# Eight products moved from GpSimd to VectorE, and the ramp's stores and a reciprocal reordered

## The chip, the cores and the metric

The kernel runs on one core of one Trainium2 chip. Its engines are TensorE (PE; its weight loads are PEld), VectorE (DVE), ScalarE (ACT), GpSimd (POOL) and SyncE (SP, which here only issues DMAs). Each works through its own list of instructions in program order and waits on semaphores for the others. The metric is the device time of one execution in microseconds (us), lower is better; several runs are given as a median.

## The reference, cut to what matters

```python
x = x + ln(attn_ref(ln(x), ...))      # x: 16 batches of 256 tokens, 128 channels
x = x + ln(ffn_ref(ln(x), ...))       # ln: layer norm without weights

def attn_ref(x, ...):                 # 8 heads of 16 channels
    Q, K, V = x @ Wq + bq, x @ Wk + bk, x @ Wv + bv
    qq, kq = Q @ Wc2q + bc2q, K @ Wc2q + bc2q             # 8 values per head
    fid = (qq @ kq.T) / maximum(norm(qq) * norm(kq), 1e-8)
    qw = fid * (1 + 0.1 * sin(fid * pi))
    aw = 0.5 * qw + 0.5 * (Q @ K.T) / sqrt(16)
    x1 = layernorm(x + (softmax(aw) @ V) @ Wo + bo, g1, beta1)
    qm = (x1 @ W1 + b1) @ Wm + bm
    ff = ((tanh(qm) * cos(qm * pi / 4)) @ Wqo + bqo) @ W2 + b2
    return layernorm(x1 + ff, g2, beta2)

def ffn_ref(x, ...):                  # 8 experts; each token goes to one
    probs = softmax(x @ gate_w); e = argmax(probs)
    return probs[e] * (gelu(x @ w1[e] + b1[e]) @ w2[e] + b2[e])
```

## The kernel before

The 4096 tokens are 32 tiles of 128, tile by tile in the partitions: 16 batches of two tiles for the attention, 8 groups of four tiles (g = 0 to 7) for the work behind it, in two halves h = 0 and 1. Every engine's program is one function, and the order of the calls in it is the order of work; nothing plans it.

**Setup and ramp.** Projections, the norms of the quantum features `u`, and for each batch b two round trips through HBM that lay operands out anew, issued from SyncE: `put_qk(b)` and `get_qk(b)` for the parts of Q and K, `put_u(b)` (four stores) and `get_u(b)` (two loads) for the features, and `put_max(b)` and `get_max(b)` for the negated maxima of the logits' rows, which TensorE needs before `logit_unit(1)` of the batch. A `get` waits until its `put` has landed. The reciprocal roots of the norms come in two parts: part 0 for batches 0 to 3, part 1 for the rest; in `reciprocals(hh)` VectorE inverts ScalarE's root (L1724), and in `root_out(hh)` GpSimd refines it in four instructions (L701 to L704) and raises `inv_h`.

**The batch loop.** For each batch VectorE runs four `weight` (L1850), two `logits` (L1880), four `top` for the batch after next (L1827) and `heads` of the batch before. TensorE's output goes round three PSUM slots, so a unit waits until the unit three places earlier is taken. GpSimd runs `split_max` (L739, L741), `split_u`, `split_qk` and a subtraction; in batch 0 `root_out(1)` stands last, and `reciprocals(1)` behind VectorE's four `top`.

**Behind the attention.** For each group g, TensorE makes the block's output, ScalarE squares it (`square_z(g)`, L1037), VectorE's `weigh(g)` (L1966, L1968) writes `t` into `u_sb`, and two sums over the channels are wanted for each token: of t squared (`square_t`, L1054, and `sum_t`) and of t times x. The product is `times_x(g)`: 128x512, into one of two buffers `tx`. For groups 0 to 3 VectorE sums it (`sum_dot(g)`, L2024); for 4 to 7 ScalarE does (`dot_x(g)`, L1063, four accumulating passes). `dots(h)` needs the sums of a half. Then VectorE makes roots (`newton`, L1996 to L1999), variances (`var_o`, L1977 to L1986), gates, the choice of the expert (`best`), places in the sorted list (`places`), and rows (`add_shift` L2012, `add_x` L2020).

**The experts.** GpSimd scatters 32 tiles of rows by indirect DMA (L828), each group when its `add_x` is done. `list_tiles` on VectorE makes the list of tiles (`exp_i`); from it ScalarE and SyncE load weights (L1173) and rows, and 23 steps of matmuls, GELU and layer norm follow.

## Time and profile before

| | |
|---|---|
| median of 3 runs | 507.27 us (504.33 to 507.42) |
| the profiled execution | 505.17 us, span 503.4 us |
| busy share of the span | PE 75%, DVE 74%, ACT 66%, POOL 49% |
| chain that ended last, by engine | DVE 39%, PE 33%, issue 11%, DMA 5%, POOL 4%, ACT 3% |
| mean granted TensorE clock | 0.884 of full speed |

The span runs from the first to the last instruction; the profiled execution's own time holds 1.77 us more. In the order of time: setup and ramp until VectorE's first `weight` at 69.65 us, batches 0 and 1 until 103.18 us, fourteen more batches until 278 us, the work behind the attention until 373.7 us, the experts until the end. In a timeline row, `[1.08 <-PE ...]` is the time that the engine had stood idle and whose work ended that; "issue" means that it waited for nothing that the profile shows. Rows of instructions that follow one another are merged (x4).

### The profile page before, as it was taken

Reading aid. Unit: us, or ns where it says so; the run is one execution under the profiler, and the core shown is the slowest. Engines: PE = TensorE matmul, PEld = TensorE weight load, DVE = VectorE, ACT = ScalarE, POOL = GpSimd, SP = SyncE. Lnnn points to the kernel's source line nnn. Section 1 sums busy time; section 2 is a strip of 40 time slices with the busy share of each in tenths; the row PEclk is TensorE's granted clock in tenths of the full one; section 3 lists DMA queues with packets and bytes.
Section 4 is the critical chain, followed back from the end, with each engine's and each line's share of the span. In section 5 each row is a group of like instructions: output and inputs, shape, how many; then the busy total and the mean of one; then the engine's idle time right before and its main releaser. Section 6 shows DMA issues by size and latency. Waiting matters only on the chain.

```text
span 503.4 us, 8868 instructions
## 1 busy us (share of the span) xinstructions
PE 377.1 (75%) x2644; PEld 264.6 (53%) x2644; DVE 372.5 (74%) x910; ACT 333.4 (66%) x635; POOL 245.3 (49%) x348
## 2 busy tenths in 40 slices
PE   1967368899999999998888898640004599999960
PEld 0755236566656666665575336440003488888840
DVE  5496587799999999999965344997982057776781
ACT  1357347699999999999866456656203287778730
POOL 7469131755555555554201224216477147766773
PEclk9998758799999999999888999976557599999995
DMA  9416344366776776676599910000128346766400
GB/s 203 16 31 158 94 90 106 97 166 165 169 174 149 175 182 170 163 170 158 143 134 146 148 22 1 2 0 23 35 73 247 106 119 198 206 208 195 136 14 0
DMA packets 87979, 60.33 MB, mean 120 GB/s; under 512 B 17213, under 2 KB 80705, under 8 KB 87926
## 3 DMA queue, kind: packets, MB, share of 16 engines
q1 hardware_dynamic: 78022, 52.07, 46.9%
q10 hardware_dynamic: 7408, 3.35, 2.7%
q0 software_dynamic: 2496, 4.29, 2.4%
q8 instruction: 23, 0.38, 0.3%
q14 instruction: 30, 0.25, 0.2%
HBM read 35.38 MB, written 25.21 MB: 120 GB/s over the span
## 4 chain that ended last, share of the span: by engine, by line
DVE 39%; PE 33%; issue 11%; DMA 5%; POOL 4%; ACT 3%; SPq 2%; ACTq 1%; POOLq 0%; DVEq 0%
DVE big L1850 11%; DVE mxs L1827 10%; PE ps L1635 8%; PE ps L1626 7%; DVE big L1880 4%; PE ps L1418 2%; PE ps L1431 2%; PE ps L1528 2%; PE ps L1523 1%; PE ps L1411 1%; PE ps L1223 1%; DVE u_sb L1889 1%; DMA qk_parts<-proj 1%; DVE gb L1698 1%; DMA uk_parts<-u_turned 1%
## 5 line engine op out<-in xcount | busy, mean ns | idle before, releaser
L1850 DVE SCALAR_TENSOR_TENSOR big<-big,ps 128x1024 f32<-128x1024 f32 x64 | 74.2, 1215 | 4.4 <-ACT big L954 4.4
L1827 DVE TENSOR_REDUCE mxs<-ps 128x4 f32<-128x1024 f32 x64 | 74.1, 1216 | 4.5 <-issue 2.8
L954 ACT ACTIVATE big<-ps 128x1024 f32<-128x1024 f32 x64 | 62.4, 1028 | 11.3 <-PE ps L1396 11.1
L842 POOL DMA_INDIRECT out_dram<-arena,fidx x46 | 46.5, 1010 | 25.3 <-DVE arena L2246 17.9
L2218 DVE TENSOR_SCALAR arena<-ps,x_all 128x128 f32<-128x128 f32 x46 | 14.0, 347 | 46.3 <-PE ps L1643 34.4
L1626 PE MATMUL ps<-arena,big 128*128 128x256 f32 x184 | 45.4, 392 | 1.1 <-issue 1.1
L1635 PE MATMUL ps<-arena,big 128*128 128x256 f32 x184 | 45.8, 393 | 0.5 <-ACT arena L1162 0.5
L1144 ACT ACTIVATE x_all<-x_all 128x128 f32<-128x128 f32 x46 | 20.3, 489 | 37.0 <-DMA x_all<-sorted_rows 30.1
L1258 PE MATMUL ps<-arena 96*128 96x256 bf16 x256 | 39.3, 285 | 7.2 <-issue 4.8
L828 POOL DMA_INDIRECT sorted_rows<-proj,sl_i x32 | 32.6, 1020 | 21.9 <-issue 15.5
L1880 DVE TENSOR_TENSOR big<-big,ps 128x1024 f32<-128x1024 f32 x32 | 37.9, 1216 | 6.9 <-PE ps L1418 6.9
L739 POOL CAST mtok<-mxs 128x16 bf16<-128x16 f32 x16 | 3.2, 198 | 81.5 <-DVE mxs L1827 81.5
L1162 ACT ACTIVATE arena<-ps,eb_sb 128x256 f32<-128x256 f32 x92 | 36.1, 475 | 7.4 <-PE ps L1626 3.7
L1626 PEld LDWEIGHTS ps<-arena,big 128*128 128x128 f32 x184 | 36.3, 198 | 7.0 <-issue 1.7
L1418 PE MATMUL ps<-arena 98*128 98x256 bf16 x256 | 38.6, 286 | 1.3 <-DMA arena<-m_parts 1.3
L1411 PE MATMUL ps<-ident,big 128*128 128x128 f32 x256 | 36.5, 288 | 2.8 <-DVE big L1850 2.5
L1431 PE MATMUL ps<-big,vb 128*32 128x256 f32 x512 | 36.9, 409 | 1.9 <-DVE u_sb L1889 1.1
L1635 PEld LDWEIGHTS ps<-arena,big 128*128 128x128 f32 x184 | 34.1, 196 | 5.5 <-ACT arena L1162 1.0
L964 ACT ACTIVATE big<-ps 128x1024 f32<-128x1024 f32 x32 | 32.8, 1024 | 6.1 <-PE ps L1418 5.9
L1411 PEld LDWEIGHTS ps<-ident,big 128*128 128x128 f32 x256 | 29.3, 146 | 9.2 <-DVE big L1850 5.9
L1258 PEld LDWEIGHTS ps<-arena 96*128 96x128 bf16 x256 | 23.0, 100 | 17.7 <-issue 14.1
L964 ACT ACTIVATE big<-big 128x1024 f32<-128x1024 f32 x32 | 32.2, 1059 | 0.0
(350 smaller groups left out, 893.0 us busy)
## 6 DMA issues: line engine op xcount, KB each, us to landing
big<-in_L_ffn_w_dram SPq DMA_DIRECT2D x34, 256.0 KB
qk_parts<-proj SPq DMA_DIRECT2D x16, 384.0 KB, 3.0
arena<-qk_parts SPq DMA_DIRECT2D x32, 192.0 KB, 3.7
sorted_rows<-zrow SPq DMA_DIRECT2D x16, 266.0 KB, 5.7
arena<-qk_parts SPq DMA_DIRECT2D x32, 128.0 KB, 3.9
big<-in_L_ffn_w_dram ACTq DMA_DIRECT2D x12, 256.0 KB
x_all<-sorted_rows SPq DMA_DIRECT2D x23, 133.0 KB
sorted_rows<-zrow SPq DMA_DIRECT2D x2, 1263.5 KB, 24.5
```

Source lines behind the costliest of these rows:

```text
L842: nc.gpsimd.indirect_dma_start(out2, bass.IndirectOffsetOnAxis(ap=fidx[:, j, t:t + 1], axis=0), fres[j][:, t, :], None, bounds_check=NT * ...
L954: nc.scalar.activation(W[par][:, n, :], src, ACT.Sin, scale=PI * (1 - 1e-6)).then_inc(sin_ready, 1)
L964: nc.scalar.activation(W[par1][:, n, :], src, ACT.Exp, scale=0.05).then_inc(p_ready, 1)
L1258: mm = nc.tensor.matmul(o[:, c:c + S], cqT[b1 % 3][0:KC, 2 * n + h, qt * P:(qt + 1) * P], ckT[b1 % 3][0:KC, 2 * n + h, :], start=True, sto ...
L1411: nc.tensor.matmul(o[:, to:to + P], W[par][:, n, at:at + P], ident[:, :], is_transpose=True, start=(kt == 0 and qt == 0), stop=False, skip ...
L1418: mm = nc.tensor.matmul(o[:, c:c + S], ckT[i3][0:KC + 2, 2 * n + h, kt * P:(kt + 1) * P], cqT[i3][0:KC + 2, 2 * n + h, :], start=not turn, ...
L1431: mm = nc.tensor.matmul(hbank[32 * j:32 * j + 32, g * S:(g + 1) * S], vb[:, b1 * TPB + kt, h * VW:h * VW + 32], W[par1][:, h // 2, c:c + S ...
L1626: mm = nc.tensor.matmul(ps[:, 1 + 2 * par + c // 2, (c % 2) * TS:(c % 2 + 1) * TS], fw1[s % DEPTH][:, c * P:(c + 1) * P], fxT[par], start= ...
L1635: mm = nc.tensor.matmul(ps[:, 5 + 2 * par, 0:TS], fw2[s % DEPTH][:, c, :], fg[par][:, c, :], start=(c == 0), stop=(c == EC - 1))
L1827: nc.vector.tensor_reduce(mxs[:, b1 % 2, :, 2 * n:2 * n + 2], src, AX_X, ALU.max, negate=True).then_inc(unit_free, 1)
L1850: nc.vector.scalar_tensor_tensor(W[par][:, n, :], W[par][:, n, :], 10.0, f, ALU.add, ALU.mult).then_inc(unit_free, 1)
L1880: nc.vector.tensor_tensor(W[par][:, n, :], W[par][:, n, :], slot_of("log", b, n), ALU.add).then_inc(unit_free, 1)
```

## The change

Four edits. On SyncE the four stores of `put_u(1)` move ahead of `get_u(0)`, and `put_qk(2)` ahead of `get_u(1)`. On VectorE `reciprocals(1)` moves from behind batch 0's `top` to ahead of its first `weight`. `times_x` becomes a VectorE instruction: the eight calls leave GpSimd's program (where six stood ahead of the scatters and two between the first four and the others) and are spread over VectorE's. On ScalarE `dot_x(4)` moves ahead of `square_t(5)` and `dot_x(5)` ahead of `square_t(6)`; `dot_x(4)` also waits until `sum_t(3)` has read the buffer that it writes to.

```diff
             put_u(0)
+            put_u(1)
             get_u(0)
-            put_u(1)
+            put_qk(2)
             get_u(1)
-            put_qk(2)
             get_qk(2)
...
-            for g in range(GH + 2):
-                times_x(g)
             pool.wait_ge(z_stored, 16 * (NB + 4))
-            scatter(0, 0, GT)
-            times_x(GH + 2)
-            times_x(GH + 3)
-            scatter(0, GT, NK)
+            scatter(0, 0, NK)
...
             def dot_x(g):
                 act.wait_ge(step["tx"], g + 1)
+                if g == GH:
+                    act.wait_ge(step["tred"], GRED[GH - 1])
...
             turn_qe(7)
+            dot_x(4)
             square_t(5)
             exps(0)
             nc.scalar.activation(hT[:, 3:4], halfpi[:, 0:1], ACT.Sqrt)
             square_z(6)
+            dot_x(5)
             square_t(6)
...
             square_t(7)
-            dot_x(4)
-            dot_x(5)
             half_root(4, 5, step["vc"], step["rc"], 1)
...
                     for n in range(HP):
                         top(1, n)
+                    reciprocals(1)
...
-                if first:
-                    reciprocals(1)
...
+            def times_x(g):
+                dve.wait_ge(step["t"], 2 * g + 2)
+                if g >= GH + 2:
+                    dve.wait_ge(step["dot"], g - GH - 1)
+                elif g >= 2:
+                    dve.wait_ge(step["tred"], GDOT[g - 2])
+                nc.vector.tensor_tensor(tx[g % 2].rearrange("p (t c) -> p t c", t=GT), t_of(g), x_all[:, g * GT:(g + 1) * GT, :], ALU.mult).then_inc(step["tx"], 1)
...
             fold(1)
+            times_x(0)
             weigh(1)
             sum_t(0)
             weigh(2)
             queries(1)
+            times_x(1)
             sum_dot(0)
...
             sum_t(2)
+            times_x(2)
             sum_t(3)
+            times_x(3)
             var_o(0)
...
             sum_dot(3)
+            times_x(4)
             dots(0)
...
             weigh(5)
+            times_x(5)
             newton(6, 7, step["rd"], 0)
...
             weigh(6)
+            times_x(6)
             weigh(7)
+            times_x(7)
             var_z(1)
```

SyncE in the ramp, from behind the stores of `put_u(0)`; the digit of a name is its buffer, here the batch, and `qk_parts0` on L499 is the store of batch 2. Before:

```order
L530 DMA proj<-uq_parts0 128x1x512
L530 DMA proj<-uk_parts0 128x1x512
L507 DMA uq_parts1<-u_turned1 64x2x256
L508 DMA uk_parts1<-u_turned1 64x2x256
L507 DMA uq_parts1<-u_turned1 64x2x256
L508 DMA uk_parts1<-u_turned1 64x2x256
L530 DMA proj<-uq_parts1 128x1x512
L530 DMA proj<-uk_parts1 128x1x512
L499 DMA qk_parts0<-proj 128x6x256
```

and now:

```order
L507 DMA uq_parts1<-u_turned1 64x2x256
L508 DMA uk_parts1<-u_turned1 64x2x256
L507 DMA uq_parts1<-u_turned1 64x2x256
L508 DMA uk_parts1<-u_turned1 64x2x256
L530 DMA proj<-uq_parts0 128x1x512
L530 DMA proj<-uk_parts0 128x1x512
L499 DMA qk_parts0<-proj 128x6x256
L530 DMA proj<-uq_parts1 128x1x512
L530 DMA proj<-uk_parts1 128x1x512
```

Both loads of the features now stand behind batch 1's stores, and the store of batch 2's Q and K stands two loads further ahead.

VectorE in batch 0 (`weight`, `logits`, `top`) and at the start of batch 1. Before:

```order
L1827 TENSOR_REDUCE mxs<-ps 128x2x2 x6
L1850 SCALAR_TENSOR_TENSOR big<-big,ps 128x1024 x4
L1880 TENSOR_TENSOR big<-big,ps 128x1024 x2
L1827 TENSOR_REDUCE mxs<-ps 128x2x2 x4
L1724 RECIPROCAL inv<-inv 128x384
L1850 SCALAR_TENSOR_TENSOR big<-big,ps 128x1024 x4
```

and now:

```order
L1816 TENSOR_REDUCE mxs<-ps 128x2x2 x6
L1713 RECIPROCAL inv<-inv 128x384
L1839 SCALAR_TENSOR_TENSOR big<-big,ps 128x1024 x4
L1869 TENSOR_TENSOR big<-big,ps 128x1024 x2
L1816 TENSOR_REDUCE mxs<-ps 128x2x2 x4
L1839 SCALAR_TENSOR_TENSOR big<-big,ps 128x1024 x4
```

The reciprocal has moved from the end of batch 0 to its beginning, ten instructions up.

VectorE behind the attention, from the last instruction of `weight_out(0)` to the first of `add_shift(1)`. Before:

```order
L2097 RECIPROCAL proj<-rs 128x16
L1966 TENSOR_TENSOR u_sb<-ps,vec_bc 128x512
L1968 COPY late_s<-ps 128x40
L1966 TENSOR_TENSOR u_sb<-ps,vec_bc 128x512
L1968 COPY late_s<-ps 128x40
L1972 SCALAR_TENSOR_TENSOR late_s<-late_s 128x16
```

and now:

```order
L2093 RECIPROCAL proj<-rs 128x16
L1954 TENSOR_TENSOR u_sb<-ps,vec_bc 128x512
L1956 COPY late_s<-ps 128x40
L2024 TENSOR_TENSOR arena<-u_sb,x_all 128x512
L1954 TENSOR_TENSOR u_sb<-ps,vec_bc 128x512
L1956 COPY late_s<-ps 128x40
L2024 TENSOR_TENSOR arena<-u_sb,x_all 128x512
L1960 SCALAR_TENSOR_TENSOR late_s<-late_s 128x16
```

A product (`arena<-u_sb,x_all`) now follows each of `weigh(6)` and `weigh(7)`; all other instructions keep their order.

## Rows read from the trace of the kernel before

**Rows 1.** Windows: stretch us, length, busy us (instructions) per engine, TensorE clock, DMA share, GB/s.

```profile
69.65:87.85 18.20, 13.85 (x98) 8.85 (x97) 14.13 (x12) 13.57 (x17) 6.40 (x10) 0.72 0.44 93
...
87.85:103.18 15.33, 12.49 (x94) 8.55 (x94) 12.03 (x13) 10.76 (x14) 10.01 (x17) 0.78 0.42 106
...
103.18:115.20 12.02, 11.43 (x114) 7.41 (x110) 11.99 (x14) 11.96 (x15) 6.51 (x12) 1.00 0.70 177
...
307.35:373.70 66.35, 22.07 (x136) 17.32 (x134) 57.14 (x204) 32.80 (x153) 28.08 (x26) 0.71 0.06 18
```

**Rows 2.** Timeline of VectorE, batches 0 and 1: start us, us, instruction, idle before.

```profile
79.73 1.22 DVE L1880 TENSOR_TENSOR big<-big,ps 128x1024 f32<-128x1024 f32 x1 [2.19 <-PE ps L1418]
...
85.39 2.54 DVE L1724 RECIPROCAL inv<-inv 128x384 f32<-128x384 f32 x1
...
93.48 1.22 DVE L1880 TENSOR_TENSOR big<-big,ps 128x1024 f32<-128x1024 f32 x1 [1.08 <-PE ps L1418]
...
96.89 1.22 DVE L1880 TENSOR_TENSOR big<-big,ps 128x1024 f32<-128x1024 f32 x1 [2.19 <-PE ps L1418]
```

**Rows 3.** Timeline of the other engines and SyncE's queue, 53 to 92 us.

```profile
53.38 0.58 SPq L530 DMA_DIRECT2D proj<-uq_parts  x1
...
60.91 0.42 SPq L499 DMA_DIRECT2D qk_parts<-proj  x1
...
69.90 0.42 SPq L536 DMA_DIRECT2D m_parts<-mrow  x1
...
75.26 1.01 PE L1418 MATMUL ps<-arena 98*128 98x256 bf16 x4 [1.29 <-DMA arena<-m_parts]
...
85.02 2.83 ACT L954 ACTIVATE big<-ps 128x1024 f32<-128x1024 f32 x3
...
88.01 0.83 POOL L701 TENSOR_TENSOR gb<-inv 128x384 f32<-128x384 f32 x1 [10.16 <-DVE inv L1724]
...
91.55 0.20 POOL L739 CAST mtok<-mxs 128x16 bf16<-128x16 f32 x1
```

**Rows 4.** Source view of the product's line on GpSimd: duration ns min/median/max.

```profile
L817 POOL TENSOR_TENSOR arena<-u_sb,x_all x8: 1263/1270/1275, 308.2 to 348.4; 128x512 f32<-128x512 f32 x8
```

**Rows 5.** Groups of VectorE from 307 to 373 us: busy us, mean ns.

```profile
L2020 DVE SCALAR_TENSOR_TENSOR proj<-u_sb,late_s,x_all 128x128 f32<-128x128 f32 x20 | 6.7, 397 | 0.1
...
L2012 DVE SCALAR_TENSOR_TENSOR u_sb<-u_sb,late_s,be2c_bc 128x128 f32<-128x128 f32 x20 | 5.6, 342 | 0.0
...
L1966 DVE TENSOR_TENSOR u_sb<-ps,vec_bc 128x512 f32<-128x512 f32 x8 | 5.4, 680 | 9.5 <-ACT gb L1037 9.5
...
L1997 DVE TENSOR_TENSOR late_s<-late_s 128x16 f32<-128x16 f32 x6 | 3.1, 521 | 0.2
...
L1999 DVE SCALAR_TENSOR_TENSOR late_s<-late_s 128x16 f32<-128x16 f32 x6 | 2.0, 334 | 0.2
...
L1985 DVE TENSOR_SCALAR late_s<-late_s,bg_bc 128x16 f32<-128x16 f32 x2 | 1.4, 712 | 0.1
...
L1945 DVE TENSOR_TENSOR late_s<-late_s,bA_bc 128x128 f32<-128x128 f32 x1 | 1.3, 1258 | 0.0
...
L1972 DVE SCALAR_TENSOR_TENSOR late_s<-late_s 128x16 f32<-128x16 f32 x2 | 1.1, 551 | 0.0
...
L1998 DVE SCALAR_TENSOR_TENSOR late_s<-late_s 128x16 f32<-128x16 f32 x6 | 1.1, 183 | 0.2
```

**Rows 6.** Timeline, 314 to 375 us, all engines.

```profile
314.20 0.69 DVE L1966 TENSOR_TENSOR u_sb<-ps,vec_bc 128x512 f32<-128x512 f32 x1 [1.82 <-ACT gb L1037]
...
341.05 0.31 ACT L1054 ACTIVATE arena<-u_sb 128x128 f32<-128x128 f32 x1 [2.62 <-DVE late_s L1968]
...
343.38 0.69 DVE L1966 TENSOR_TENSOR u_sb<-ps,vec_bc 128x512 f32<-128x512 f32 x1 [2.36 <-ACT gb L1037]
...
360.87 0.96 POOL L828 DMA_INDIRECT sorted_rows<-proj,sl_i  x1 [5.17 <-DVE proj L2020]
...
374.71 0.39 ACTq L1173 DMA_DIRECT2D big<-in_L_ffn_w_dram  x1
```

More of the change, by code:

```diff
@@ L809, in _ @@
             std_y(1)
-            def times_x(g):
-                pool.wait_ge(step["t"], 2 * g + 2)
-                if g >= GH + 2:
-                    pool.wait_ge(step["dot"], g - GH - 1)
-                elif g >= 2:
-                    pool.wait_ge(step["tred"], GDOT[g - 2])
-                nc.gpsimd.tensor_tensor(tx[g % 2].rearrange("p (t c) -> p t c", t=GT), t_of(g), x_all[:, g * GT:(g + 1) * GT, :], ALU.mult).then_inc(step["tx"], 1)
             def scatter(k, lo=None, hi=None):
```

## Prediction

> **What bounds the kernel now.** I first cut the span into stretches with the windows view, to see which engine fills each. A regular batch, the one from 103.18 to 115.20 us, takes 12.02 us and keeps VectorE busy for 11.99 of them and ScalarE for 11.96, with TensorE at its full clock [rows 1]. The two batches before it are longer, 18.20 and 15.33 us, though VectorE's work in them is 14.13 and 12.03 us, and TensorE's granted clock is 0.72 and 0.78 of full speed there, between its two levels of 1.2 and 2.4 GHz. So in the ramp VectorE waits. Behind the attention, from 307.35 to 373.70 us, VectorE is busy 57.14 of 66.35 us and every other engine under half: the stage is one chain on VectorE. The change touches these two places.
>
> Next I read VectorE's timeline in the ramp for what it waits for. In batch 0 it waits 2.19 us for the logits from TensorE, and at the end it spends 2.54 us on the reciprocal. In batch 1 it waits 1.08 and 2.19 us, both for TensorE's logits [rows 2]; these 3.27 us are nearly all of the 3.31 by which batch 1 exceeds a regular one. The other engines tell why. In batch 0, TensorE's first logit unit waits for the row maxima from HBM until 75.26 us, whose store SyncE issued at 69.90, behind the long queue of loads. In batch 1, GpSimd begins `root_out(1)` at 88.01, having idled 10.16 us for the reciprocal, and only then, at 91.55, starts `split_max(2)`, which batch 1's first logit unit needs [rows 3].
>
> Behind the attention I looked for VectorE instructions that take longer than their shape asks for. The product on GpSimd takes 1.27 us, eight times [rows 4]. In the same stretch small VectorE instructions have means far above those of like shape [rows 5]; in the timeline each of the long ones lies under a GpSimd product and ends with it.
>
> **The change, part by part: the ramp.** *SyncE.* The store of batch 2's Q and K, issued at 60.91 us, comes 7.53 us behind the first load of `get_u(0)` at 53.38 [rows 3], with four stores, a wait for their landing and two loads between. Now `get_u(0)` goes behind the four stores, later by at most 4 x 0.58 = 2.3 us (0.58 is the row of the load; a store is taken alike), and the Q and K store follows its two loads: at 53.38 + 2.3 + 1.2 = 56.9 at the latest, 4.0 us sooner. The loads that wait for it, and behind them the store of the maxima, come sooner by as much: that store at about 65.9 instead of 69.90, and the maxima are in SBUF at some 71.3 instead of 75.26. `get_u(0)` and `get_u(1)` feed cosine units over ten and twenty us later, so their own moves cost nothing; with that cover gone, they would cost those 2.3 us.
>
> *The reciprocal in batch 0.* It now stands ahead of the first `weight`: 2.54 us on the path there, from 69.65 to about 72.2. Queued behind it are the four weights, and TensorE and ScalarE wait for those. Nothing else is late at its wait, since the root that it reads was made before the batches began. With four weights of about 1.14 (the pace of a full queue) VectorE is through them at 76.7. The logits of heads 2 and 3 need only the second weight's slot, free at about 74.5, and the maxima, which are in: TensorE starts there 0.7 us sooner than at 75.26. The next unit needs the third weight's slot, at 75.6. Before, that unit began at 75.26 + 1.01 = 76.27, so VectorE's second wait ends at 79.73 - 0.6 = 79.1. The reciprocal thus goes into waiting time, and what is late next is still TensorE. From there to batch 1 it was 87.85 - 79.73 = 8.12 us, of which 2.54 is the reciprocal: 5.58 remain, and batch 1 could start at 84.7. But its first `weight` needs ScalarE's first sine, which began at 85.02 [rows 3] and moves by the same 0.6, and takes 0.94 (2.83 for three): 85.4. So batch 1 starts 2.4 us sooner. Bounds: 1.8 (the sine doesn't move) and 3.1 (VectorE alone decides).
>
> *Batch 1.* GpSimd's `root_out(1)`, which filled 88.01 to 91.55, now falls into its 10.16 us of idleness, and `split_max(2)` is done as soon as the maxima are. That takes away the wait of 1.08 us. The second one, 2.19, has TensorE working through its logits at the reduced clock; with no gap ahead of it I expect most of it to go too. Bounds are 0 (something else is just as late) and 3.3 (a regular batch); I take 2.6, nearer to the regular batch, since nothing in its row looks different from batch 1's but the clock. The ramp together: 2.4 + 2.6 = 5.0, between 1.8 and 6.4.
>
> **The change behind the attention.** *What goes.* The excess of the long instructions over like shapes, from [rows 5]: L1945 1.258 - 0.342 = 0.92; L1972 2 x (0.551 - 0.183) = 0.74; L1997 6 x (0.521 - 0.183) = 2.03; L1999 6 x (0.334 - 0.183) = 0.91; L1985 2 x (0.712 - 0.183) = 1.06, of which I take 1.0; L2020 20 x (0.397 - 0.342) = 1.10. Together 6.7 us. The first, 0.92, lies ahead of VectorE's wait of 1.82 us for ScalarE [rows 6], so only what ScalarE itself gains reaches the path: 0.3, my estimate between 0 and 0.92. The others, 5.8, are on the path. *What comes.* Eight products of 128x512 on VectorE. The nearest row is `weigh`'s own product of this shape, 0.68 us, with one operand in PSUM. I take 0.65, because unhindered neighbours overlap a little; ends 0.6 and 0.78, the latter with a wait for the instruction just ahead. Product 0 falls into the wait of 1.82 us and product 6 into that of 2.36 us, both for `square_z` on ScalarE [rows 6], and cost nothing; without that cover 0.65 each. Six are on the path: 3.9 us. Net gain 0.3 + 5.8 - 3.9 = 2.2; ends 5.8 - 4.7 = 1.1 and 0.9 + 5.8 - 3.6 = 3.1.
>
> The Trainium skill, "VectorE: DVE Perf Modes", section on the TRN2 errata, gives a float32 product of two tensors as (N + 151) cycles at 0.96 GHz, 0.69 us here. By it the six would cost 4.1 and this part would gain 2.0. The trace's nearest row, 0.68, agrees with it.
>
> *ScalarE.* `dot_x(4)` and `dot_x(5)` are four passes of about 0.3 us each, 1.2 us. The second falls into ScalarE's idle 2.62 us ahead of `square_t(6)` [rows 6], the first into a like gap ahead of `square_t(5)`. Products 6 and 7 wait for them with `weigh(7)` queued behind; both should be done. In exchange ScalarE's last four dot sums become two, so `dots(1)` doesn't wait. *GpSimd.* The scatters lose nothing: group 2 waits 5.17 us for VectorE's rows at 360.87, and comes sooner by what VectorE gains. The weight loads at 374.71 follow VectorE's list [rows 6], so the experts move up whole.
>
> **The sum.** 5.0 + 2.2 = 7.2 us. Against the profiled execution, 505.17, that gives 498.0; against the median, 507.27, it gives 500.1. Two of the three runs lie at 507.3, one at 504.3, so I take the middle: **499 us**.
>
> **Rivals.** *Batch 1 stays long.* TensorE's granted clock is 0.78 there, and if it stays so after the ramp's idleness, batch 1 keeps its second wait or finds another. VectorE's reciprocal now holds TensorE up just ahead of batch 0's logits. For it speaks the reduced clock in both batches, against it that the gap caused by GpSimd goes. Then the ramp gives 2.4 and the whole 4.6: 501.6 us. 0.20. The Trainium skill, "TensorE: Matmul & The Clock Gate", Part 1, says that the clock is set by how busy the array has been recently. By that rule the trace agrees: 0.72 with TensorE busy 13.85 of 18.20 us, 1.00 with 11.43 of 12.02 [rows 1].
>
> *The products cost what the stalls cost.* If all eight are on VectorE's path at 0.78 us (6.2) this stage gains nothing, and 5.0 remain: 501.2 us. Against it speak the two waits of [rows 6]. 0.12.
>
> *The ramp does nothing.* VectorE, TensorE and ScalarE stand still for some us at the start of batch 0 for the branch between the two bodies of the loop; the earlier store now runs beside what they fetch. If that takes 4 us longer, or batch 0 loses by the reciprocal what batch 1 gains, only 2.2 remain: 504 us. 0.08.
>
> *Slower.* The reciprocal's 2.54 us are not covered, TensorE stays at its lower clock for a further batch, and the third batch takes 15.33 instead of 12.02: +2.5 + 3.3 - 2.2 = +3.6, 509.7 us on the same middle. It decides from the point where the windows of the third batch show a clock near 0.78. Against it speaks that a regular batch holds TensorE busy 11.4 of 12 us. 0.05.
>
> **Chances and range.** My forecast has 0.55. A measurement of this kernel tells about 1% from no change, 5.1 us: faster means under 502.2. The forecast lies there but for a twentieth, and most of the first two rivals do: 0.52 + 0.12 + 0.09 is 0.73 for faster; 0.23 for the same; 0.04 for slower. The range goes from 495.5 (6.4 + 3.1 off the profiled execution) to 504, which takes in the first two rivals and leaves out the last and half of the third.
>
> **What would show it.** In the windows of the changed kernel: batch 0 at about 15.8 us, batch 1 at 12 to 13 with a clock near 1.00, no wait for GpSimd's `split_max(2)`. In VectorE's groups: L1997 back at 0.18 us, the product at 0.6 to 0.7, the two waits for `square_z` shorter by a product each. From the first `weigh` to the list some 64 us instead of 66.35. The forecast is wrong if batch 1 stays above 14 us, or if the products make VectorE late for an engine that now waits for nothing.

## The result, and the profile after

The changed kernel takes 501.99 us (median of 8 runs, 499.75 to 504.29), the kernel before on the same chip 506.95 (8 runs, 504.33 to 509.47). The ratio is 0.9894 with a 95% interval of 0.9868 to 0.9919: 5.4 us off, between 4.1 and 6.7. Forecast were 499.0 in a range of 495.5 to 504.0, from a sum of 7.2 off; the measured gain lies on the side that had 0.73, but it is only just over 1%, and its interval begins at 0.8%. The profiled execution took 503.79 us (span 502.1).

The windows of the changed kernel over batches 0, 1 and 2 and from the first `weigh` to the list, with the columns of [rows 1]:

```profile
70.01:86.12 16.11, 13.81 (x82) 8.74 (x81) 13.98 (x12) 11.90 (x15) 10.15 (x17) 0.67 0.24 58
86.12:98.08 11.96, 11.27 (x112) 7.33 (x110) 11.92 (x12) 11.90 (x15) 6.35 (x11) 1.00 0.67 169
98.08:110.04 11.96, 11.40 (x114) 7.41 (x110) 11.93 (x13) 11.90 (x15) 6.41 (x12) 1.00 0.69 167
305.22:370.10 64.88, 24.92 (x136) 20.36 (x134) 55.35 (x212) 32.78 (x153) 18.34 (x18) 0.69 0.06 18
```

Batch 0 takes 16.11 us where 15.8 was forecast and batch 1 is a regular batch at full clock; the third batch starts at 98.08 instead of 103.18, 5.1 us sooner, though batch 0 began 0.36 us later. The stretch behind the attention is shorter by 1.47 us, not 2.2. The engines in the ramp, from the timeline of the changed kernel, where L1713 is the reciprocal, L1869 `logits`, L1816 `top` and L701 `root_out`:

```profile
62.25 3.49 DVE L1816 TENSOR_REDUCE mxs<-ps 128x4 f32<-128x1024 f32 x3 [5.17 <-PE ps L1247]
...
70.00 2.54 DVE L1713 RECIPROCAL inv<-inv 128x384 f32<-128x384 f32 x1
...
78.16 0.82 POOL L701 TENSOR_TENSOR gb<-inv 128x384 f32<-128x384 f32 x1
...
79.65 1.22 DVE L1869 TENSOR_TENSOR big<-big,ps 128x1024 f32<-128x1024 f32 x1 [1.51 <-PE ps L1407]
...
85.57 0.20 POOL L739 CAST mtok<-mxs 128x16 bf16<-128x16 f32 x1 [3.82 <-DVE mxs L1816]
...
90.66 2.35 DVE L1869 TENSOR_TENSOR big<-big,ps 128x1024 f32<-128x1024 f32 x2
```

GpSimd does `root_out(1)` from 78.16 in its idle time, `split_max(2)` starts at 85.57 instead of 91.55, and in batch 1 neither `logits` waits (90.66); the waits of 1.08 and 2.19 us of [rows 2] are gone. But the first row, ahead of batch 0, shows something that was not forecast: VectorE stands idle for 5.17 us. The row names TensorE, but by the program this `top` takes a unit that TensorE had finished at 56.67 us, so the label doesn't tell what VectorE waited for. SyncE's queue and the copy that makes the row of maxima, from the same timeline:

```profile
53.34 0.58 SPq L530 DMA_DIRECT2D proj<-uq_parts  x1
...
54.60 0.42 SPq L499 DMA_DIRECT2D qk_parts<-proj  x1
...
65.63 0.36 ACT L902 COPY mrow<-ps 16x256 bf16<-16x256 bf16 x1 [9.51 <-PE ps L1238]
...
66.02 0.30 SPq L536 DMA_DIRECT2D m_parts<-mrow  x1
```

The store of batch 2's Q and K is issued 6.3 us sooner than before and the store of the maxima 3.9 us sooner [rows 3]; 4.0 was worked out for both. For the maxima the agreement is luck. SyncE had issued the loads ahead of that store by 64.08, and the store goes out when ScalarE's copy ends, which the 5.17 us have made late. VectorE's groups behind the attention (busy us, mean ns; L2008 is `add_x`, L2024 now the product, L1985 and L1987 belong to `newton`):

```profile
L2008 DVE SCALAR_TENSOR_TENSOR proj<-u_sb,late_s,x_all 128x128 f32<-128x128 f32 x20 | 5.7, 348 | 0.1
...
L2024 DVE TENSOR_TENSOR arena<-u_sb,x_all 128x512 f32<-128x512 f32 x8 | 5.5, 686 | 0.1
...
L1987 DVE SCALAR_TENSOR_TENSOR late_s<-late_s 128x16 f32<-128x16 f32 x6 | 1.0, 175 | 0.2
L1985 DVE TENSOR_TENSOR late_s<-late_s 128x16 f32<-128x16 f32 x6 | 1.0, 174 | 0.2
```

And the rows of its timeline there that have a wait, two of `weigh` and one of `newton`:

```profile
312.24 0.69 DVE L1954 TENSOR_TENSOR u_sb<-ps,vec_bc 128x512 f32<-128x512 f32 x1 [2.36 <-ACT gb L1024]
...
317.18 0.25 DVE L1984 RECIPROCAL late_s<-late_s 128x16 f32<-128x16 f32 x1 [0.45 <-ACT late_s L1063]
...
341.14 0.69 DVE L1954 TENSOR_TENSOR u_sb<-ps,vec_bc 128x512 f32<-128x512 f32 x1 [1.63 <-ACT gb L1024]
```

The long small instructions of [rows 5] are back at 174 and 175 ns, and a product takes 0.69 us. The wait at `weigh(7)` has shrunk from 2.36 to 1.63, by one product, as forecast. The wait at `weigh(2)` has grown from 1.82 to 2.36 [rows 6], and one of 0.45 us for `half_root` is new.

Three questions follow. Do the edits of the ramp each do what was said? What is the stand of 5.17 us? And is the smaller gain behind the attention the products' doing?

### The profile page after: what moved, and what is told of

Same layout as the page of the kernel before. It is cut to its first block, busy times and chain, and to the rows that moved or that the text cites. A ratio compares the mean times of both kernels' runs of the same rounds, so it can differ in the third digit from the quotient of the medians.

```text
span 502.1 us, 8869 instructions
## 1 busy us (share of the span) xinstructions
PE 384.6 (77%) x2644; PEld 269.5 (54%) x2644; DVE 370.4 (74%) x918; ACT 332.8 (66%) x635; POOL 235.3 (47%) x340
## 4 chain that ended last, share of the span: by engine, by line
DVE 43%; PE 33%; issue 9%; ACT 6%; POOL 3%; DMA 3%; ACTq 2%; POOLq 0%; SPq 0%; DVEq 0%
DVE big L1839 12%; DVE mxs L1816 11%; PE ps L1624 6%; PE ps L1615 6%; DVE big L1869 5%; DMA x_all<-sorted_rows 2%; PE ps L1420 2%; PE ps L1512 2%; PE ps L1212 2%; PE ps L1517 2%; PE ps L1543 1%; PE ps L1544 1%; DVE u_sb L1878 1%; DVE gb L1687 1%; POOL out_dram L834 1%
## 5 line engine op out<-in xcount | busy, mean ns | idle before, releaser
L1816 DVE TENSOR_REDUCE mxs<-ps 128x4 f32<-128x1024 f32 x64 | 74.0, 1216 | 6.0 <-PE ps L1247 6.0
L1615 PE MATMUL ps<-arena,big 128*128 128x256 f32 x184 | 47.4, 404 | 1.7 <-issue 1.2
L1624 PE MATMUL ps<-arena,big 128*128 128x256 f32 x184 | 45.8, 393 | 1.0 <-ACT arena L1151 0.8
L1615 PEld LDWEIGHTS ps<-arena,big 128*128 128x128 f32 x184 | 37.4, 205 | 8.1 <-issue 2.5
L1869 DVE TENSOR_TENSOR big<-big,ps 128x1024 f32<-128x1024 f32 x32 | 37.8, 1216 | 3.0 <-PE ps L1407 3.0
L1624 PEld LDWEIGHTS ps<-arena,big 128*128 128x128 f32 x184 | 34.2, 196 | 6.0 <-ACT arena L1151 1.3
```

The lines of the kernel that those rows point to most:

```text
L1615: mm = nc.tensor.matmul(ps[:, 1 + 2 * par + c // 2, (c % 2) * TS:(c % 2 + 1) * TS], fw1[s % DEPTH][:, c * P:(c + 1) * P], fxT[par], start= ...
L1624: mm = nc.tensor.matmul(ps[:, 5 + 2 * par, 0:TS], fw2[s % DEPTH][:, c, :], fg[par][:, c, :], start=(c == 0), stop=(c == EC - 1))
L1816: nc.vector.tensor_reduce(mxs[:, b1 % 2, :, 2 * n:2 * n + 2], src, AX_X, ALU.max, negate=True).then_inc(unit_free, 1)
L1869: nc.vector.tensor_tensor(W[par][:, n, :], W[par][:, n, :], slot_of("log", b, n), ALU.add).then_inc(unit_free, 1)
```

## The experiments

The first theory was that the two parts add up: some 5 us in the ramp, of which SyncE's order is worth one, and 1.5 behind the attention. A change in us is (ratio - 1) times the median of the kernel before in the same runs (507.0 to 508.6). By "stand" I mean VectorE's idle time between its last instruction ahead of the branch into batch 0 and its first behind it.

**The four parts alone**, each an edit of the kernel before. `e1_sp_only`:

```diff
             put_u(0)
+            put_u(1)
             get_u(0)
-            put_u(1)
+            put_qk(2)
             get_u(1)
-            put_qk(2)
```

> The kernel before with SyncE's new order alone. Theory (two parts that add up: the ramp about 5 us, the work behind the attention about 1.5 us): the store of batch 0's maxima comes some 4 us sooner, so the 2.19 us wait for the logits in batch 0 shrinks, but the reciprocal still stands at that batch's end and GpSimd's root_out(1) still delays batch 1: -1.2 us, between 0 and -2.2; batch 1 stays at about 15. Rival A (the order of the stores is the ramp's whole gain): -5 us and a batch 1 of about 12. Rival B (SyncE's order decides nothing, because TensorE is held by its clock or by the slots): 0.

Measured: 1.0018 (0.9995 to 1.004), 0.9 us slower, -0.3 to +2.0. In the profile batch 0 does get shorter, 16.1 us, but it starts 2.5 us later, because of this stand (timeline of VectorE); batch 1 stays at 14.9, as expected, and the third batch starts at 103.19, as before:

```profile
64.42 3.49 DVE L1827 TENSOR_REDUCE mxs<-ps 128x4 f32<-128x1024 f32 x3 [7.24 <-issue]
...
72.18 2.34 DVE L1850 SCALAR_TENSOR_TENSOR big<-big,ps 128x1024 f32<-128x1024 f32 x2
```

The theory of a gain of 1.2 falls. `e2_recip_only` moves `reciprocals(1)` alone:

```diff
                     for n in range(HP):
                         top(1, n)
+                    reciprocals(1)
...
-                if first:
-                    reciprocals(1)
```

> The kernel before with reciprocals(1) ahead of batch 0's weights, nothing else. Theory: GpSimd does root_out(1) in its idle time and split_max(2) is ready, so batch 1 becomes a regular batch of about 12 us with the clock near 1.00 (-3), and batch 0 loses 2.54 us of VectorE's work at its end but starts its weights later, with the maxima as late as before: -1 to -2.4 there; together -4.4 us. Rival A (the stores' order is the ramp's gain): 0 to -1 us. Rival C (each needs the other: the reciprocal is only covered if the maxima come early): batch 0 gains nothing, -2.5 us.

Measured: 0.9919 (0.9889 to 0.9949), 4.1 us off. Batches 0 and 1 in its windows:

```profile
68.90:85.79 16.89, 13.29 (x82) 8.56 (x81) 13.98 (x13) 11.89 (x15) 10.09 (x17) 0.68 0.36 85
85.79:97.75 11.96, 11.32 (x114) 7.33 (x110) 11.93 (x12) 11.90 (x15) 6.40 (x11) 1.00 0.73 171
```

With the maxima as late as before, the reciprocal alone brings the third batch to 97.75, 5.4 us sooner; 0.75 of that is an earlier start. Rival A falls. So does C, whose 2.5 us lie just outside the interval (2.6 to 5.6), since batch 0 gained too: 16.89 us with the reciprocal in it, instead of 18.20. `e3_ramp` has both edits:

> The kernel before with both edits of the ramp, the products still on GpSimd. Theory: -5.0 us, of a total of -5.4 to -6.5; the stretches behind the ramp as in the kernel before. Rival (the ramp's gain is given back later, because earlier stretches run at other clocks): the profile shows batches 0 and 1 shorter by 5, and the time falls by 3 or less.

Measured: 0.9953 (0.9933 to 0.9973), 2.4 us off, less than the reciprocal alone on the same chip. Its reciprocal starts at 71.20 instead of 68.90, its batch 0 takes 16.06; the third batch starts at 99.22, 4.0 us sooner than before. The expected 5.0 is missed. Of the 2.6 that are missing, 1.7 lie between the two runs, which differ in the order of the stores alone; their intervals overlap. The rival, that a part of the gain is given back later, is not excluded by this run. `e4_products` has the products on VectorE, the two `dot_x` moved on ScalarE, the scatters in one call, and the ramp as before.

> The kernel before with the products on VectorE and the dot sums sooner on ScalarE, the ramp as before. Theory: -1.5 us, which is what the stretch from the first weigh to the list showed in the profiles of before and after (66.35 to 64.88). As forecast: -2.2 us. Rival (the products cost what the stalls cost, and the experts take back the rest): 0. Rival (the whole gain of the change beyond the ramp is lost at the experts, whose first steps then find weights or rows missing): 0 with a stretch of about 64.9 and a longer start of the experts.

Measured: 0.996 (0.9938 to 0.9983), 2.0 us off; both rivals of 0 fall. From the first `weigh` to the list its stretch takes 63.78 us, 2.6 less than before [rows 1]:

```profile
308.25:372.03 63.78, 22.42 (x136) 17.66 (x134) 55.26 (x212) 32.75 (x153) 18.34 (x18) 0.72 0.06 19
```

So the 64.88 of the changed kernel was no property of the products; `e10_after_old_sp`, below, has the same products and takes 63.77. Of the difference of 1.1 us, 1.0 are two waits: 0.55 more ahead of `weigh(2)`, and the 0.45 for `half_root`, which `e4_products` doesn't have. The windows of 5.4 us from `weigh(1)` on, of the changed kernel:

```profile
308.50:313.90 5.40, 5.40 (x34) 5.32 (x32) 3.00 (x9) 3.79 (x14) 0.00 (x0) 0.68 0.00 0
```

and of `e4_products`:

```profile
311.50:316.90 5.40, 4.50 (x35) 3.89 (x34) 3.56 (x10) 5.32 (x22) 0.00 (x0) 1.00 0.00 0
```

TensorE's granted clock is 0.68 in the one and 1.00 in the other, for the same matmuls; at the lower clock TensorE is the last to be ready for `square_z(2)`, and the gap ahead of `weigh(2)` is 2.36 us instead of this one:

```profile
314.72 0.69 DVE L1955 TENSOR_TENSOR u_sb<-ps,vec_bc 128x512 f32<-128x512 f32 x1 [1.81 <-ACT gb L1024]
```

In this place the clock is 0.68 in three of the fourteen profiles (the changed kernel, `e3_ramp` and `e5_pool_tiny`) and 1.00 in the others. `e3_ramp` has its products on GpSimd, so it is not VectorE's products that lower it.

**Why batch 1 was long.** `e9_root_late` moves only GpSimd's `root_out(1)`:

```diff
             def body(b, par, first, last, slow):
                 if not last:
                     split_max(b + 1)
+                if b == 1:
+                    root_out(1)
...
-                if first:
-                    root_out(1)
```

> The kernel before with GpSimd's root_out(1) moved from the end of batch 0 to batch 1, behind split_max(2); nothing on VectorE or SyncE is moved. Theory (batch 1 is long because split_max(2) is queued behind root_out(1), which waits for the reciprocal): batch 1 falls from 15.3 to 12 to 13 us, batch 0 stays at 18.2, the time falls by 2.5 to 3.3. Rival (batch 1 is long because TensorE's granted clock is low after batch 0): batch 1 stays above 14.5 and the time within 0.8 of before.

Measured: 0.995 (0.9931 to 0.9968), 2.5 us off. The windows of batches 1 and 2:

```profile
87.73:99.76 12.03, 10.13 (x94) 7.00 (x94) 11.93 (x14) 10.52 (x14) 9.82 (x15) 1.00 0.37 103
99.76:114.80 15.04, 12.65 (x112) 8.82 (x110) 12.15 (x12) 12.01 (x15) 6.30 (x11) 0.89 0.70 172
```

and what TensorE waits for in batch 2, from its timeline:

```profile
107.35 1.49 PE L1258 MATMUL ps<-arena 96*128 96x256 bf16 x8 [1.86 <-DMA arena<-qk_parts]
```

Batch 1 is regular, at full clock, though nothing on VectorE, SyncE or TensorE was moved: the queue on GpSimd made it long, and the low clock came with the wait. The rival falls. But now `split_qk(4)` is queued behind `root_out(1)`, the loads of batch 4's Q and K come later, and batch 2 takes 15.04. The two nearly cancel in the profile; the median kept 2.5 us, which that one profile doesn't explain.

**The order of the stores.** `e10_after_old_sp` is the changed kernel with SyncE's lines as before.

> The changed kernel with SyncE's old order. Theory, after the runs of the parts (the new order lets the loads of Q and K of batch 2 run while VectorE stands at the branch into batch 0, which then takes 5.2 to 7.2 us instead of 2.8): VectorE stands there for about 2.8 us again, reaches the reciprocal near 69.0, batch 0 takes some 16.9, batch 2 starts near 97.8; the time is 1 to 2 us below the changed kernel, so 6.4 to 7.4 below the kernel before. Rival (the two profiles differ by chance, the new order is worth the 0.7 of the forecast): 0.7 slower than the changed kernel, 4.7 below before.

Measured: 0.9863 (0.9839 to 0.9886), 7.0 us off, as the theory has it. Against the changed kernel's 0.9894 the intervals overlap; but `e1_sp_only` against before, `e3_ramp` against `e2_recip_only` and this pair, the last across chips, give 0.9, 1.7 and 1.6 us, all to the same side, though none is clear of noise by itself. Its stand is 3.00 us, but here the time ahead of the branch ran 1.1 us longer, so the third batch starts no sooner in this profile, at 98.45.

What makes the stand long? I first suspected the loads of batch 2's Q and K. `e11_qk_behind_max` is the changed kernel with those loads held back:

```diff
             put_qk(2)
             get_u(1)
-            get_qk(2)
             put_max(0)
             get_max(0)
+            get_qk(2)
```

> The changed kernel with SyncE's get_qk(2) behind get_max(0): the stores keep the new order, but the loads of Q and K of batch 2 no longer run while VectorE stands at the branch. Theory: the stand takes about 3 us, the reciprocal comes near 69, the maxima are in before TensorE wants them, batch 0 takes 15.8 to 16.1, batch 2 starts near 96.8; 1.3 to 2.5 us below the changed kernel, 6.7 to 8 below before. Rival (VectorE's long stand has nothing to do with those loads): it stays above 5 us and the time equals the changed kernel's, 5.4 below before.

Measured: 0.9895 (0.9871 to 0.9919), 5.3 us off, equal to the changed kernel; the stand is 5.42 us. That theory falls, as the rival expected. Next the store itself: `e12_zero_store` puts a store of zeros into the old order.

```diff
             get_u(0)
+            zeros(6)
             put_u(1)
```

> The kernel before with a store of 408 KB of zeros (one that SyncE issues later anyway) put between get_u(0) and put_u(1), so that it runs where the store of batch 2's Q and K (384 KB) runs in the new order. In six profiles with the old order VectorE stood 2.7 to 3.3 us at the branch into batch 0, in four with the new one 5.2 to 7.2, also where the loads behind that store were held back. Theory (a store under way makes the stand longer, whatever it carries): 4.5 us or more, the first weight at 71 or later, the time 0 to 2 above before. Rival (the stand depends on the order of the loads of the features, not on a store): 2.7 to 3.3.

Measured: 1.0028 (1.0008 to 1.0049), 1.4 us slower, and the stand is 4.73 us:

```profile
62.90 3.49 DVE L1828 TENSOR_REDUCE mxs<-ps 128x4 f32<-128x1024 f32 x3 [4.73 <-issue]
```

Stores in this place lengthen it too, and the rival falls; which stores is not settled, since the zeros also push `put_u(1)` later, so that the next load goes out at 62.48 instead of 59.68. The first weight moves only 1.0 us, to 70.66, since before, too, VectorE waited for TensorE just behind the stand. Part of the 1.4 us may come from what else was queued behind the zeros: the maxima are stored 2.3 us later. `e13_store_held` removes the store from that place. It stands on `e7_covers_old_sp`, further below, with the order put_u(0), put_u(1), get_u(0), get_u(1), put_max(0), get_max(0), put_qk(2), get_qk(2).

> The run with the new places under waits, with another order on SyncE: both put_u, both get_u, then put_max(0) and get_max(0), and only then put_qk(2) and get_qk(2). Theory (the store of Q and K makes VectorE's stand long): no store runs there, the stand is 2.7 to 3.3 us, the reciprocal comes near 68.3; the maxima are in early, so batch 0 takes 16.0 or less unless the loads of batch 2's Q and K, now some 6 us later, make its last top late: 498 to 501. Rival (the stand is long because both put_u come first): it stays above 5 us.

Measured: 0.9875 (0.9833 to 0.9917; four runs between 496.96 and 503.79), 6.3 us off. The stand is 5.51 us without the store, as the rival said, so the store cannot be the only cause. Against `e7_covers_old_sp` itself, which is 10.8 us off, this order loses 4.5, across chips. The windows of single microseconds tell more. The kernel before, and then the same of `e13_store_held` (the last column is GB/s):

```profile
59.00:60.00 1.00, 0.00 (x0) 0.00 (x0) 0.00 (x0) 0.00 (x0) 0.00 (x0) 0.50 0.08 24
60.00:61.00 1.00, 0.00 (x0) 0.00 (x0) 0.00 (x0) 0.00 (x0) 0.00 (x0) 0.50 0.00 0
```

```profile
59.00:60.00 1.00, 0.00 (x0) 0.00 (x0) 0.00 (x0) 0.00 (x0) 0.00 (x0) 0.50 0.27 94
60.00:61.00 1.00, 0.00 (x0) 0.00 (x0) 0.00 (x0) 0.00 (x0) 0.00 (x0) 0.50 0.27 92
```

Before, SyncE's wait for `put_u(1)` to land leaves the DMA engines nearly empty from 59 to 61 us. In the new orders something always runs there, in this one the loads of the features. The view of DMA traffic also shows two packets of a queue called "instruction", in the kernel before between 59 and 60 us (packets, MB, share of the 16 engines):

```profile
q14 instruction: 2, 0.02, 5.1%
```

and in the changed kernel between 60 and 61, beside 77 packets of others:

```profile
q1 hardware_dynamic: 77, 0.07, 23.9%
q14 instruction: 2, 0.02, 3.9%
```

VectorE goes on 1 to 2 us after them, at 61.01 and 62.25. So the stand looks like the fetch of the code behind the branch, delayed by the traffic beside it. `e14_quiet` tests that: like `e13_store_held`, but `get_u(1)` also waits behind `get_max(0)`.

> The run with the new places under waits, with this order on SyncE: both put_u, get_u(0), put_max(0), get_max(0), get_u(1), put_qk(2), get_qk(2). Since get_u(1) now waits behind put_max(0), which VectorE's first maxima after the branch release, nothing that SyncE issues runs from about 57 us until VectorE is past the branch. Theory, mended after the held store left a stand of 5.5 us (not the store alone but any transfer under way makes the stand long; before, the wait for put_u(1) left 59 to 61 us without traffic): the stand is 3.3 us or less, the reciprocal comes near 68, batch 0 takes about 15.6, batch 2 starts near 95.5; 497 to 499 us on a chip where before takes 507.4. Rival (the stand is long because put_u(1) comes ahead of get_u(0), whatever runs): 5 us or more, the reciprocal at 70, 499 to 501.

Its timeline, with VectorE's first instruction behind the branch and TensorE's wait in batch 0:

```profile
61.53 1.23 DVE L1816 TENSOR_REDUCE mxs<-ps 128x4 f32<-128x1024 f32 x1 [3.33 <-issue]
...
81.01 1.89 PE L1247 MATMUL ps<-arena 96*128 96x256 bf16 x8 [1.37 <-DMA arena<-qk_parts]
```

and its windows, of one quiet microsecond and of batch 0 with the reciprocal:

```profile
60.00:61.00 1.00, 0.00 (x0) 0.00 (x0) 0.00 (x0) 0.00 (x0) 0.00 (x0) 0.50 0.00 0
...
69.61:88.98 19.37, 16.06 (x78) 10.29 (x77) 14.07 (x12) 11.90 (x15) 9.88 (x15) 0.55 0.58 132
```

The stand is 3.33 us with both `put_u` in front, so the rival falls, and it is the traffic that goes with a long stand. That holds over all fourteen profiles. In eight of them the windows from 1.5 to 2.5 us into the stand show 0 GB/s, and the stand is 2.72 to 3.33 us; in the other six they show 75 to 93 GB/s, and it is 4.73 to 7.24. TensorE, which stands at the same branch, doesn't follow this rule. Its rows before and in the changed kernel:

```profile
61.97 1.86 PE L1258 MATMUL ps<-arena 96*128 96x256 bf16 x8 [4.85 <-issue]
```

```profile
60.78 1.87 PE L1247 MATMUL ps<-arena 96*128 96x256 bf16 x8 [4.11 <-issue]
```

Its stand, the idle time of these rows, is 3.82 to 5.51 us in the eight profiles and 4.11 to 5.95 in the six. So that a fetch of code is what the traffic delays stays a reading of the records, not a finding. The time of `e14_quiet`, though, is 0.9891 (0.987 to 0.9911), 5.5 us off: the loads of batch 2's Q and K, held back to 74.62, are now late for batch 0 itself, TensorE waits, its clock stays at 0.55, and batch 0 takes 19.37 us. The expected 497 to 499 is missed for this reason.

**The prices behind the attention.** `e5_pool_tiny`; both lines are shortened, and `G` stands for `0:(C if g < 2 else 1)`:

```diff
-tensor_tensor(tx[g % 2], t_of(g), x_all[:, g * GT:(g + 1) * GT, :], ALU.mult)
+tensor_tensor(tx[g % 2][:, :, G], t_of(g)[:, :, G], x_all[:, g * GT:(g + 1) * GT, G], ALU.mult)
```

> The kernel before with GpSimd's products 2 to 7 cut to one channel of 128, so that the dot sums of groups 2 to 7 are of old values; the first two are whole. It prices the stalls alone. The six long instructions under these products exceed their like by 0.77 + 1.08 + 0.96 + 1.02 + 0.96 + 0.77 = 5.6 us. Theory (they are stalls that GpSimd's reads cause, and lie on VectorE's path): each is back at 0.17 to 0.35 us, the stretch from the first weigh to the list falls from 66.2 by 4.5 to 5.6 (some of it turns into waits for ScalarE), the time by 4.5 or more. Rival (the long instructions wait for something else): their durations stay, the time stays.

Measured: 0.9896 (0.9859 to 0.9932), 5.3 us off. The groups of VectorE, where L1945, under the whole product 0, is the control:

```profile
L1945 DVE TENSOR_TENSOR late_s<-late_s,bA_bc 128x128 f32<-128x128 f32 x1 | 1.3, 1255 | 0.0
L1999 DVE SCALAR_TENSOR_TENSOR late_s<-late_s 128x16 f32<-128x16 f32 x6 | 1.1, 176 | 0.2
...
L1997 DVE TENSOR_TENSOR late_s<-late_s 128x16 f32<-128x16 f32 x6 | 1.0, 175 | 0.2
L1985 DVE TENSOR_SCALAR late_s<-late_s,bg_bc 128x16 f32<-128x16 f32 x2 | 0.5, 234 | 0.1
```

and the window from the first `weigh` to the list:

```profile
307.19:369.49 62.30, 24.06 (x136) 19.44 (x134) 51.58 (x204) 32.68 (x153) 21.71 (x26) 0.70 0.06 19
```

They were stalls, and GpSimd's products made them; the edit cuts their reads and their writes alike. Since the dot sums are of old values, the experts may get other rows, so the price is the stretch, not the time. But of 5.6 us of stalls only 4.1 left the stretch (66.35 to 62.30): VectorE now waits 0.67 us for `half_root`, 0.39 for the dot sums, and 0.33 more ahead of `weigh(2)`. The first and the last of these go with the clock: the changed kernel has the same two waits, and from `weigh(1)` on `e5_pool_tiny` has the changed kernel's clock of 0.68 (first window), while the kernel before ran at 1.00 there (last window):

```profile
310.82:316.22 5.40, 5.40 (x32) 5.10 (x31) 3.21 (x10) 4.04 (x15) 1.27 (x1) 0.68 0.00 0
...
319.15 0.25 DVE L1996 RECIPROCAL late_s<-late_s 128x16 f32<-128x16 f32 x1 [0.67 <-ACT late_s L1074]
```

```profile
310.99:316.39 5.40, 4.11 (x32) 3.49 (x31) 3.54 (x10) 5.23 (x21) 1.40 (x2) 1.00 0.00 0
```

**A better order.** `e7_covers_old_sp` is `e10_after_old_sp` with work moved under waits. VectorE:

```diff
+            times_x(1)
+            sum_dot(0)
+            queries(1)
             weigh(2)
-            queries(1)
-            times_x(1)
-            sum_dot(0)
             sum_t(1)
+            sum_dot(1)
             var_z(0)
             weigh(3)
-            sum_dot(1)
+            times_x(2)
+            times_x(3)
             newton(2, 3, step["rb"], 0)
             sum_t(2)
-            times_x(2)
             sum_t(3)
-            times_x(3)
...
             times_x(6)
+            add_shift(1)
             weigh(7)
-            times_x(7)
             var_z(1)
-            add_shift(1)
+            times_x(7)
```

and on ScalarE `half_root(2, 3, ..., 0)` goes ahead of `wide_square_t(2)`, and `dot_x(6)` ahead of `half_root(4, 5, ..., 1)`.

> The changed kernel with SyncE's old order and its new instructions placed under waits: product 1, the dot sum of group 0 and queries(1) ahead of weigh(2), which waits 2.36 us; the dot sum of group 1 ahead of weigh(3); products 2 and 3 ahead of the newton that waits 0.45 us; add_shift(1) ahead of weigh(7), which waits 1.63 us; var_z(1) ahead of product 7; on ScalarE the first half_root ahead of the square of group 2, and dot_x(6) ahead of the last half_root(4, 5). Theory (the shortfall behind the attention is new waits ahead of weigh(2) and newton, which such work can fill): 2.4 us below the run with the old order alone, from the first weigh to the list 62.3 instead of 64.7. Rival (TensorE's pace ahead of square_z(3) and square_z(7) is late next, so work put there only moves the wait): 0 to -0.8.

Measured: 0.9787 (0.9763 to 0.9811), 498.57 us where the kernel before took 508.59: 10.8 us off, and clearly faster than both kernels and than `e10_after_old_sp`, by 3.9 us. The window of its stretch:

```profile
305.28:366.27 60.99, 22.99 (x136) 18.49 (x134) 55.26 (x212) 32.48 (x153) 18.37 (x18) 0.70 0.06 20
```

and the one wait for ScalarE that is left there, from VectorE's timeline:

```profile
338.40 0.69 DVE L1954 TENSOR_TENSOR u_sb<-ps,vec_bc 128x512 f32<-128x512 f32 x1 [0.59 <-ACT gb L1024]
```

VectorE's busy time is the 55.26 of `e4_products`, and the stretch is 2.8 us shorter than there and than in `e10_after_old_sp`: all of it waits that were filled, somewhat more than the expected 2.4. The rival falls.

## Why the prediction was right, and where it was off

**The reciprocal and batch 1: right.** Forecast were 2.4 us in batch 0, of which 0.6 hung on SyncE's order, and 2.6 in batch 1; alone, the edit gives 4.1 (2.6 to 5.6). Batch 1 became a whole regular batch (3.4 us, where the upper bound was 3.3), and `e9_root_late` shows that GpSimd's queue was the cause. The rival "batch 1 stays long" had the clock as the cause; in [rows 1] the clock of 0.78 was a consequence of the wait.

**SyncE's order: the step that failed.** The text said that the own moves of `get_u(0)` and `get_u(1)` "cost nothing" and let the earlier maxima bring 0.6 us. The maxima did come 3.9 us sooner, and batch 0 is shorter by it: 16.06 us in `e3_ramp` against 16.89 in `e2_recip_only`. But the old order had a nearly empty stretch, the wait for `put_u(1)` to land, exactly while VectorE stood at the branch. With transfers in it the stand is 5.17 instead of 2.83 us, and the order costs 0.9 to 1.7 us in all, by the three comparisons above. The third rival named this mechanism, at 4 us and with 0.08; it came in at part of that. The term of 5.0 for the ramp held in the one profile (5.1), where VectorE came to the branch 1.1 us sooner than before and batch 1 gave more than forecast, and not in the times (`e3_ramp`: 2.4, 1.4 to 3.4): that agreement is luck. The Trainium skill, "DMA: Bandwidth & Descriptors", section "Issuing engines are not separate DMA queues", says that DMAs started by ScalarE, SyncE or GpSimd run on the same 16 DMA engines and interleave. No run here shows it, since SyncE issued all the transfers in question; that a fetch of code is among them is only inferred, from the "instruction" packets.

**Behind the attention: right, term by term, at the clock of the kernel before.** Forecast was 2.2, measured alone 2.0 (0.9 to 3.1), and the stretch of `e4_products` is 2.6 shorter, at the same granted clock ahead of `weigh(2)`. The half "what goes" was 6.1: in the two timelines the six long instructions behind `weigh(2)` shrink by 5.8 together, and `weigh(2)` starts 6.47 us behind the first `weigh` instead of 6.85, 0.38 where 0.3 was forecast. The half "what comes" was 3.9: six products put off what follows them by 0.60 to 0.72 us each, 3.9 together. Product 0 cost nothing, since VectorE still waits 1.81 us for `square_z(2)` behind it, and product 6 fell into its wait (2.36 to 1.63). The 1.47 of the changed kernel's profile and the 4.1 of `e5_pool_tiny` are too small by what the lower clock cost there, 1.0 us each. The duration of a product, 0.69, was right; back to back they follow every 0.60 us (two in 1.28). The Trainium skill, "SBUF — State Buffer", section "Who interferes with whom", says that a VectorE instruction with two SBUF inputs contends with a GpSimd one that reads SBUF, and that the one that starts later is blocked. The trace agrees: L1945 takes 1.26 us under a product and 0.29 in `e4_products`, L1997 1.25 and 0.18.

**The experts: not to be read from one pair of profiles.** The span fell by 1.3 us only, though the third batch started 5.1 sooner. Batches 13 to the end of the attention's loop took 42.54 us before and 44.22 after; in the fourteen profiles this stretch takes 42.4 to 42.5 five times, 44.1 to 44.2 five times, and more four times, and TensorE's mean clock in it is 0.88 at 42.5, 0.85 at 44.2 and 0.78 at 46.7 (`e10_after_old_sp`). The four profiles with SyncE's lines and the reciprocal as before are all among the five short ones; of the ten with either changed only `e13_store_held` (42.41) is. One execution each doesn't show whether the ramp moves the place at which the clock falls, so the rival of `e3_ramp`, that a part of the ramp's gain is given back later, stays open. From there to the first `weigh` three profiles take 30.7 and eleven about 32.0; from the list to the end they lie between 128.3 and 132.5. What a change gains upstream is seen in the medians, not in the end of one profile.

What stays open: what VectorE waits for at the branch, and why the traffic lengthens its stand and not TensorE's; why `e9_root_late` kept 2.5 us; what sets the place at which the clock falls, and whether the ramp moves it.

## What to carry to other kernels

Before filling an idle stretch of the DMA queues, look at what else may use it: here it lay at a branch into new code, and with transfers in it the engine on the critical path stood 2 us longer. Compare the price of a removed stall, or of the work that replaces it, between profiles with the same granted clock: here waits that go with the clock are worth 1.0 us, as against the 1.47 that the first pair of profiles showed. Then place the new work under the waits that are left, which here took 2.8 us more off the stretch, as much again as the change behind the attention. An instruction moved past a queue should be followed to all that stands behind it, as `root_out(1)`, moved by one batch, moved the wait by one batch in the profile.

## What the runs showed of the hardware that was not expected

- A stand of VectorE at a branch of 2.7 to 3.3 us where no DMA traffic ran from 1.5 to 2.5 us into it, and of 4.7 to 7.2 us beside 75 to 93 GB/s, be it loads or stores. TensorE's stand at the same branch shows no such difference.
- In the same stretch of 5.4 us, with the same matmuls, TensorE was granted 0.68 in three executions and 1.00 in eleven; the lower clock moved two waits of VectorE by 0.55 and 0.45 us.
- A tensor-scalar instruction with only one tensor as its operand (L1985, 128x16) was also held by a GpSimd product, 1.19 instead of 0.23 us.
